# One core, latent attention over 12,544 context rows: the 98 context tiles in steps of 2, 23 times 4, 2 and 2

## The reference, cut to what matters

```python
# x: (1, 128, 256); ctx: (1, 12544, 256); all fp32
q = layernorm(x)
a = softmax(ctx @ q.T, axis=-1)      # (12544, 128): over the 128 latents, for each context row
x = x + a.T @ ctx                    # (128, 256): summed over all 12544 context rows
x = x + causal_attention(layernorm(x), 16 heads)
x = x + layernorm(x) @ W.T + b + (layernorm(x) @ V_r) @ C.T
```

## Time and profile before

| | |
|---|---|
| median of 3 runs | 107.16 us (107.12 to 107.17) |
| the profiled execution | 107.33 us, of which its trace spans 105.3 us |
| busy share of the span | PE 95%, PEld 84%, DVE 73%, ACT 69%, POOL 60% |
| granted TensorE clock | full (2.4 GHz) in all slices but the last |
| loaded from memory | 27.6 MB, of it 25.7 MB context |

### The profile page before, as it was taken

How to read it: one execution, slowest core, us unless ns; L and a number is a source line. 1 busy time by engine, 2 the same in 40 slices (tenths; PEclk the granted TensorE clock), 3 DMA queues, 4 the chain that set the end, 5 groups by cost and what they waited for, 6 DMA issues and landing times.

```text
span 105.3 us, 2285 instructions
## 1 busy us (share of the span) xinstructions
PE 100.6 (95%) x757; PEld 88.2 (84%) x757; DVE 76.6 (73%) x217; ACT 72.7 (69%) x267; POOL 62.8 (60%) x44
## 2 busy tenths in 40 slices
PE   6799999999999999999999999999999999999990
PEld 1289999999999999999999999999999958857660
DVE  0513999978897778977778877778879865699431
ACT  4019999779997788777798777797779507399220
POOL 6406999959999767866668866668868020000020
PEclk9999999999999999999999999999999999999999
DMA  3999999999999999999999999981000000000001
GB/s 72 331 408 417 417 404 409 400 412 406 412 403 406 408 411 409 409 411 400 412 406 415 403 408 406 378 304 40 0 0 0 6 0 0 0 0 6 0 0 50
DMA packets 8746, 27.86 MB, mean 265 GB/s; under 512 B 1120, under 2 KB 1824, under 8 KB 8736
## 3 DMA queue, kind: packets, MB, share of 16 engines
q1 hardware_dynamic: 8736, 27.73, 67.3%
HBM read 27.59 MB, written 0.13 MB: 263 GB/s over the span
## 4 chain that ended last, share of the span: by engine, by line
PE 75%; issue 15%; DVE 3%; DMA 2%; POOL 1%; POOLq 1%; DVEq 0%
PE bank L312 42%; PE bank L324 20%; PE bank L327 10%; DMA x<-x_dram 2%; PE bank L333 1%; POOL rstd L274 1%; DVE bn L583 1%; PE bank L336 1%; PE bank L296 1%; POOLq L58 1%; DVE rstd_diag L590 1%; DVE x L731 0%; DVE x L659 0%; DVE mean_var L584 0%; PE bank L343 0%
## 5 line engine op out<-in xcount | busy, mean ns | idle before, releaser
L282 POOL TENSOR_TENSOR rows_split<-rows_ring,rows_split 128x1024 fp32r<-128x1024 f32 (+1 forms) x25 | 58.4, 2334 | 18.2 <-ACT rows_split L492 18.2
L312 PE MATMUL bank<-query_t,cols_ring 128*128 128x128 f32 x392 | 47.7, 275 | 0.0
L312 PEld LDWEIGHTS bank<-query_t,cols_ring 128*128 128x128 f32 x392 | 45.7, 192 | 1.4 <-ACT query_t L483 0.3
L503 ACT ACTIVATE bank<-bank,neg_max 128x128 f32<-128x128 f32 x98 | 33.1, 338 | 11.3 <-DVE neg_max L620 11.0
L324 PE MATMUL bank<-rows_split,probs 128*128 128x512 f32 x92 | 34.9, 414 | 0.0
L492 ACT CAST rows_split<-rows_ring 128x1024 fp32r<-128x1024 f32 (+1 forms) x25 | 25.9, 1034 | 3.6 <-DMA rows_ring<-ctx_rows_dram 3.0
L637 DVE SCALAR_TENSOR_TENSOR probs<-bank,inv_sums,probs 128x128 fp32r<-128x128 f32 x98 | 27.6, 344 | 0.9
L327 PE MATMUL bank<-rows_split,probs 128*128 128x256 f32 x92 | 25.6, 279 | 0.0
L620 DVE TENSOR_REDUCE neg_max<-bank 128x4 f32<-128x512 f32 (+1 forms) x25 | 16.9, 675 | 11.9 <-PE bank L312 11.6
L324 PEld LDWEIGHTS bank<-rows_split,probs 128*128 128x128 f32 x92 | 17.4, 189 | 3.0
L503 ACT ACTIVATION_READ_ACCUMULATOR bank<-bank,neg_max 128x1 f32 x98 | 19.8, 202 | 0.0
(11 more groups left out here) (90 smaller groups left out, 65.8 us busy)
## 6 DMA issues: line engine op xcount, KB each, us to landing
cols_ring<-ctx_cols_dram SPq DMA_DIRECT2D x24, 512.0 KB, 14.8
rows_ring<-ctx_rows_dram SPq DMA_DIRECT2D x24, 512.0 KB, 15.3
wqk_sb<-w_qk_dram SPq DMA_DIRECT2D x1, 512.0 KB, 9.9
cols_ring<-ctx_cols_dram SPq DMA_DIRECT2D x1, 256.0 KB, 10.9
rows_ring<-ctx_rows_dram SPq DMA_DIRECT2D x1, 256.0 KB, 10.4
wv_sb<-w_v_dram SPq DMA_DIRECT2D x1, 256.0 KB, 10.3
wproj_sb<-w_proj_dram SPq DMA_DIRECT2D x1, 256.0 KB, 10.2
wffn_sb<-w_ffn_dram SPq DMA_DIRECT2D x1, 256.0 KB, 9.7
```

The costliest lines, as they stand in the source:

```text
L282: pool.tensor_tensor(rows_split[:, b, 0:n, 1, :], rows_ring[:, slot * STEP:slot * STEP + n, :], rows_split[:, b, 0:n, 0, :].bitcast(F32), ...
L312: last = pe.matmul(into[:, t * P:(t + 1) * P], cols_ring[:, slot * STEP + t, c, :], query_t[:, c, :], start=(c == 0), stop=(c == DC - 1))
L503: last = act.activation(on[:, t * P:(t + 1) * P], on[:, t * P:(t + 1) * P], ACT.Exp, bias=neg_max[:, b, t:t + 1], accum_out=sums[:, b, t:t ...
```

## The change

The steps are cut anew: 26 steps, of which step 0 and the last two (24 and 25) have 2 tiles and the 23 between have 4 (2 + 92 + 2 + 2 = 98). The first tile of a step is now a sum (`first_of`), since it is no longer 4 s. Nothing else is edited. But all that is written in steps goes over to the new ones: `LAG`, the depth of the rings, the slots (a slot of a 2-tile step is half filled), the turn of the banks, and `ENDING`, whose last two steps now hold 4 tiles where they held 6.

```diff
-    STEPS = -(-TILES // STEP)
+    SHORT = 2
+    assert TILES % STEP == SHORT
+    STEPS = TILES // STEP + 2
...
     def tiles_of(s):
 
-        return min(STEP, TILES - s * STEP)
+        return SHORT if s == 0 or s >= STEPS - 2 else STEP
+
+    def first_of(s):
+
+        return sum(tiles_of(i) for i in range(s))
...
-                             ctx_cols[:, s * STEP * D:(s * STEP + n) * D]).then_inc(cols_landed[slot], 16)
+                             ctx_cols[:, first_of(s) * D:(first_of(s) + n) * D]).then_inc(cols_landed[slot], 16)
...
-                             ctx_rows[:, s * STEP * D:(s * STEP + n) * D]).then_inc(rows_landed[slot], 16)
+                             ctx_rows[:, first_of(s) * D:(first_of(s) + n) * D]).then_inc(rows_landed[slot], 16)
```

## The result

The changed kernel took 107.96 us (median of 6 runs, 107.73 to 108.54), the kernel before 107.25 beside it (6 runs, 107.12 to 107.48): a ratio of 1.0062, with a 95% interval of 1.0041 to 1.0082. The forecast was 106.99 in a range of 106.82 to 107.38. Both the sign and the range were wrong. The profiled execution took 108.02 us with a span of 106.0, 0.7 more than before in both.

The account below looks back on a forecast made before the run. PE, busy for 95% of the span, was taken to bound the kernel. -0.26 (slip ahead of score 3) + 0.11 (slip ahead of score 4) - 0.02 (ending form) = -0.17 us, from 107.16 to 106.99, range 106.82 to 107.38.

Parts of the forecast that it names:

- part 1: On PE, steady steps: step size costs nothing by itself; only the ending form changes, by -0.02 us.
- The place of a half load: In the DMA stream: h, the time a 256 KB load takes behind the one before, taken as 0.70 us against 1.28 full.
- Rival (a): At the start: half loads cost by their bytes, h = 0.64, score 4 not late; -0.28 us, 106.88; chance 0.12.
- cols 3 near 10.35: Sign at the start: cols 3 lands near 10.35 us and score 3 starts without a wait near 10.45.
- cols 3 lands at 11.51 - 2 (1.28 - h): At the start: two halved loads ahead of cols 3 bring its landing forward, each by 1.28 less h.
- -0.26, slip ahead of score 3: At the start: PE's existing stall before score 3 goes, winning 0.26 us.
- +0.11: At the start: score 4 is late by 0.11 us, waiting for cols 4.
- the tail: End of the load stream: its last, half-size cols load showed a place of 0.71 us, with 0.1 of rounding.
- Rival (c): At the start: half loads are dear while rings fill, cols 4 late by 2h - 1.29, kernel slower; chance 0.12.
- (d): At the start: the first score doesn't start sooner, since query_t releases it; held true and contained in the sum.
- parts 2 and 3: Softmax at weigh 1 has 0.65 us in hand, the last normalize at the end 0.5; neither costs anything.
- N: Theory from the experiments: the number of DMAs in the queue's first microseconds, not their size, makes the slow loads.

Follow-up runs that it names:

- the late halves: Kernel before with cols 6 and rows 6 each loaded by two DMAs of 2 tiles, the first loads whole: 107.56 us against 107.56, 0.999.
- the third short step: Kernel before with steps of 4 (23 times), then 2, 2, 2, its head unchanged: 107.84 us against 107.48, 1.003.
- the merged kernel: The changed kernel with cols 0 and cols 1 loaded by one DMA of 6 tiles: 1.0001 against the kernel before, in a second set 0.9974.
- the cut by tile: Kernel before with cols 0 and rows 0 each loaded by two DMAs of two tiles (2 KB per partition): 109.22 us against 107.48, 1.0176.
- The cut across partitions: Kernel before with its first loads each cut into two DMAs of 64 partitions by four tiles, pieces still 4 KB: 110.67 us against 107.48, 1.0291.

## Why the prediction was wrong

**What bounds the kernel, and the cost on PE (part 1): right.** After has steps of 3.18, the tiles of the ending form cost 0.35 each (83.85 to 84.20 above), and nothing else grew. The piece behind x1 kept its length: +0.71 at x1, +0.7 in the span.

**The place of a half load: right where it was read, and read for the wrong question.** The forecast took 0.70 from the last cols; rows 0 had 0.66, the late halves 0.69. Rival (a)'s 0.64 was as near. So none of the three things that the prediction named as signs of its being wrong came about: no half load over 0.8, no wait for `probs`, no change behind x1. What failed is on its list of what would show it, cols 3 near 10.35.

**The step that failed: cols 3 lands at 11.51 - 2 (1.28 - h).** It lets each load at the head be worth its own place and nothing more. Cols 3 was due at 10.35 and landed at 11.30; cols 4 was due at 12.94 and landed at 13.85. Each is 0.9 late, and the 0.9 is all in one place: cols 2, the full load behind the half one. The term "-0.26, slip ahead of score 3" became +0.52 (0.78 against 0.26 of before), the "+0.11" ahead of score 4 became +0.09, and 0.19 ahead of score 2 was not in the sum at all: together +0.80. All rows behind h came from the tail, where 10.9 us lie between issue and landing; at the head there are 4 to 6. The runs show that this distinction decides: the same two cuts cost nothing behind a long backlog (0.999) and 1.8% at the head.

**Rival (c) had the side and its sum, not the mechanism.** It let a half load be dear itself, and gave +0.43 for h = 1.0 and +0.99 for 1.28. Cols 4 landed 0.25 earlier than before; by its formula, 2 (1.28 - h) = 0.25, that is h = 1.155, which gives -0.28 + 1.02 = +0.74, close to the 0.71. I gave it 0.12 because of the tail's row. Rival (a) itself spoke of smaller packets that fill the engines less at the very start; that should have kept the tail from being used against (c). No row of the trace of before shows a small context load at the head, so its cost was bounded from one side only.

**The page's rule.** The Trainium skill (Perfetto Trace Analysis, DMA Optimizations) prefers larger DMAs for bandwidth. It pointed to the right side. Its step from 2 KB to 4 KB alone is not what the runs show: 2 KB pieces behind a backlog moved at 389 GB/s against 406 and cost nothing, and two extra loads of 4 KB at the head cost 0.7% with all context loads in pieces of 4 KB. The same section says that splitting may let work start sooner where the DMA engines are idle. They weren't: their share was 1.02 already in before from 4.0 us on, and what (d) says, that the first score doesn't start sooner, held: 5.92 against 5.96.

**The softmax beside it and the end (parts 2 and 3): right.** No wait of PE for `probs` stands in the waits of after, and the last normalize ended 0.5 ahead of its weigh, as forecast. That this margin is real is shown by the third short step, which used it up and 0.2 more.

**The forecast of the gain itself** is borne out only where the dip is taken away: 0.29 less from first score to x1 in two of four profiles of the merged kernel, against the 0.28 of rival (a), the case in which no load is late. In the medians it shows as nothing in one set and 0.26% in the other.

**What stays open.** What makes a few packets last long in the dip, some of them over a microsecond, is not shown. Up to 5.0 us SP spends 0.43 to 0.64 us on each issue in both kernels, and a load's place is 1.28, so it isn't SP's own instruction. In the five executions with a dip (the change twice, the cut by tile, the two runs with 4 KB loads) the stretch from 5.5 to 7.0 us is the slowest of the three from 4.0 to 8.5 (345, 309, 255, 298 and 265 GB/s), whichever load is then mostly under way: cols 2, cols 2, cols 1, rows 0 and cols 1. So "the load behind the small one" may be the wrong name for what is hit. A supply between issue and engines that has no reserve yet would fit that fewer DMAs take the dip away. The engines' share fell to 0.86 to 0.88 in that stretch of the 4 KB loads and of the cut loads, which fits it too, but stayed at 1.0 in that of the change, which doesn't; that one 4 KB load costs twice what two cost isn't explained by it, and of the two runs with the change and a second issuing engine one has no dip and one has low rates. This supply is argued and not shown. Nor is the number of DMAs told from their size. The change issues as many as before up to 3.6 us, only smaller ones, so N as I put it doesn't cover the change itself. The runs with a cut or with 4 KB loads issue more and smaller ones for the same bytes, and the merged kernel fewer and a larger first one. All dips have a small load among the first loads, but so has the merged kernel, in its rows 0, and it has no dip. The cut across partitions, which was to keep the pieces whole, has no profile at full clock.

## What to carry to other kernels

A duration holds for the place from which it is read: take the price of a load at the kernel's start from rows at the start, and where there are none, leave the bad end of the range wide. At the start of a kernel like this one, don't make loads smaller or more numerous to start sooner without a trace of it; look at the landing times of the full loads behind them, not at that of the small one. A short first step did no harm here once its load came together with the next one's, and won at most 0.3%.

## What the runs showed of the hardware that I had not expected

- One 4 KB load behind the first context load moved the landing of the next from 6.41 to 7.96 and the kernel by 1.5%.
- In the dip the packets of 4 KB keep their median of 159 ns; 15 of 241 last over 0.3 us, up to 1.46.
- Loads on 64 of 128 partitions went with 202 GB/s against 412, at an engine share of 1.03, in an execution of 170.13 us at a low granted clock.
- Loads from ACT's queue don't go ahead of those that SP has issued earlier (2.87 to 9.97), and delay SP's x if they are issued at the same time (2.79 to 4.09).
- PE's pace after the first score differs between executions of the merged kernel, 56 loads in 6.36 to 6.71 us, at a granted clock that reads 1.00, and the first score's start scatters from 5.96 to 6.41 in the kernel before.
